# Moving VectorE's picks behind the wide maxima and ScalarE's widening behind the scores in a graph attention kernel

## The chip, the cores and the metric

The kernel runs on one core of one Trainium2 chip. The metric is the device time of one execution in microseconds, and the median over several runs is what counts. PE is TensorE, DVE is VectorE, ACT is ScalarE, POOL is GpSimd and SP is SyncE; a line such as L2286 is that line of the kernel before.

## The reference

A graph of 12,500 nodes and 212,500 edges (self loops included, edges sorted by destination) passes through one attention layer with two heads and edge features, and then through three plain attention layers. The change is in the plain layers and in a judgement made once before them. A plain layer computes:

```python
h = x @ W
alpha_s = h @ a_src
alpha_d = h @ a_dst
e = alpha_s[src] + alpha_d[dst]
e = jnp.where(e > 0, e, NEG_SLOPE * e)
m = jax.ops.segment_max(e, dst, num_segments=n_nodes)
...
ex = jnp.exp(e - m[dst])
s = jax.ops.segment_sum(ex, dst, num_segments=n_nodes)
alpha = ex / (s[dst] + 1e-16)
out = jax.ops.segment_sum(alpha[:, None] * h[src], dst, num_segments=n_nodes)
return out + b
```

It adds a self loop per node, and a ReLU stands between the layers. The last layer's result is added to a residual.

## The kernel before, in words

**The units.** Each plain layer is the function `plain_layer`, called three times with tables of 67 columns (one that holds 1, 64 features, and the source and destination scores). The edges are cut into units. A unit covers up to 128 consecutive destination nodes and 16 tiles of 128 edges. Its 16 tiles of source rows come in two ways. Four tiles are "kept": one is the unit's own rows (self loops), three hold edges whose source lies among the first 1920 nodes, which rest in SBUF as bfloat16 pieces. The other twelve tiles are fetched by POOL, one indirect DMA of 128 rows each (L2150).

**The picks.** For the kept tiles VectorE builds matrices of zeros and ones from a list of places: `make_picks` compares the list with the node numbers (L2221) and with five block numbers (L2223). TensorE multiplies them with the own rows (L2430) and the pieces (L2434), and ScalarE copies the product into the row buffer (`copy_classes`, L2342). The picks have two buffers, used in turn; the semaphore `picks_used` says that TensorE has read one.

**The round.** Units run in a loop of rounds of four, with a ring of four row buffers. In the round of unit n VectorE goes through these steps, in this written order:

1. `localize` for unit n+2 (L2197) and `build_mask` for unit n+1 (L2203, L2205);
2. the picks for unit n+1 (L2221, L2223);
3. `finish` for the unit two before (L2232 to L2238, in the last layer L2244) and `begin` for unit n (L2261 to L2270);
4. `weigh` for unit n: the maximum over tiles (L2277, L2278, then after the last scores L2280, L2281, L2282), the carried sums (L2251), the leaky step over all 2048 scores (L2286), the unit's maxima made wide (L2290 to L2293), the rescale difference (L2296), and, once TensorE has turned the wide maxima (`max_turned`, L2496), the subtraction of the maximum in three parts (L2300).

ScalarE in the same round widens the destination scores of unit n+2 (`widen_er`, L2336), copies the kept rows (L2342), makes twelve tiles of scores after the first eight gathers and four after the last four (L2363), copies the turned result (L2349), and takes the exponentials behind each part of the subtraction (L2393, L2395). TensorE turns the widened scores (`turn_er`, L2411), spreads edges over destinations (L2419), sums the weighted rows (L2464), and multiplies the picks of unit n+1 after the first eight tiles of its sums.

POOL only gathers: before each unit it waits until the sums of the unit four before are made and the indices are there. SP loads each unit's lists four units ahead, one after the other in one queue.

**The judgement.** While the two-headed layer runs, VectorE lists the edges in 116 fitting units (`Arrangement`). `write_classes` marks per partition whether one of four counts is too large (L1224), TensorE sums the marks over the partitions, and `judge` (L1249 to L1256) sets which list of units the plain layers run: `plain_base`, the first unit, and `plain_last`, the last. The long list that fits any graph has 128 times 139 units.

Of the kernel before, what the change touches and what calls it, by code (L numbers as in the profile page):

```python
# [24 lines left out]
P = 128  # L25
# [4 lines left out]
NB = P  # L30
# [902 lines left out]
class Arrangement:  # L933
# [22 lines left out]
    def place(self, ctx):  # L956
        def sb(tag, shape, dt=F32):
            return ctx.enter_context(self.nc.sbuf_tensor(f"arr_{tag}", shape, dt))
        sem = self.con.sem
        self.tiles = [sb(f"tile{k}", [P, CAP], I32)[:, :] for k in range(4)]  # L960
        self.counts = [sb(f"counts{k}", [P, 3 * BANK * 2], F16)[:, :] for k in range(2)]
        self.loc_out = sb("loc_out", [P, KEPT * P], F16)
        self.first, self.prior, self.span, self.spare = (sb(tag, [P, 1]) for tag in ("first", "prior", "span", "spare"))
        self.first_raw, self.after_raw, self.prior_raw = (sb(tag, [P, 1], I32) for tag in ("fr", "ar", "pr"))
        self.kept, self.left = (sb(tag, [P, 1]) for tag in ("kept", "left"))
        self.bad, self.met = sb("bad", [P, 4]), sb("met", [1, 4])
        self.to_far = sb("to_far", [P, 1])
        self.class_counts = sb("class_counts", [P, KEPT])
        self.class_most = sb("class_most", [P, 1])
        self.near_ints, self.near_floats = sb("near_ints", [P, INTS], I32), sb("near_floats", [P, FLOATS])  # L970
        self.late_ints = sb("late_ints", [P, self.later, INTS], I32)
        self.late_floats = sb("late_floats", [P, self.later, FLOATS])
        self.nice = sb("nice", [1, 1])
        self.rows_loaded, self.late_loaded = sem("arr_rows_loaded"), sem("arr_late_loaded")
        self.late_made, self.late_stored, self.chain = sem("arr_late_made"), sem("arr_late_stored"), sem("arr_chain")
        self.bad_made, self.bad_summed = sem("arr_bad_made"), sem("arr_bad_summed")
# [229 lines left out]
    def write_classes(self, ve):  # L1206
# [5 lines left out]
        for k in range(KEPT):  # L1212
# [6 lines left out]
        step(ve.scalar_tensor_tensor(temp, temp, self.to_far[:, 0:1], valid, ALU.add, ALU.mult))  # L1219
        step(ve.tensor_scalar(self.tiles[3][:, 0:KEPT * P].rearrange("r (k p) -> r k p", k=KEPT), temp,  # L1220
                              float(self.far), None, ALU.add))
        for k, (count, most) in enumerate(((self.kept, LISTED - 1), (self.left, SLOTS), (self.class_most, P),
                                           (self.span, NB - 1))):
            step(ve.tensor_scalar(self.bad[:, k:k + 1], count[:, :], float(most), None, ALU.is_gt))  # L1224
        ve.sem_inc(self.bad_made, 1)

    def beside(self, ve, n):
# [20 lines left out]
    def judge(self, ve, ps_bad):  # L1248

        step, nice = self.step, self.nice[:, :]  # L1250
        ve.wait_ge(self.bad_summed, 1)
        for k in range(4):
            step(ve.tensor_scalar(self.met[:, k:k + 1], ps_bad[:, k:k + 1], 0.0, float(4 << k), ALU.is_gt, ALU.mult))
        step(ve.tensor_reduce(nice, self.met[:, :], AX.X, ALU.add))
        step(ve.memset(self.con.plain_base[:, :], 0))
        step(ve.tensor_scalar(self.con.plain_last[:, :], nice, float(SETS - 1), None, ALU.add))  # L1256

    def store(self, gp, stored):

# [29 lines left out]
def heads_layer(nc, con, name, units, src, dst, table, out, middle, edge_attr, attn_l, w_out, arrange):  # L1289
# [17 lines left out]
    with ExitStack() as ctx:  # L1307
# [107 lines left out]
        with nc.Block() as block:  # L1415
# [114 lines left out]
            def _(ve):  # L1530
# [158 lines left out]
                weigh_rows(n, RING - 1, weighted_last)  # L1689
                finish(n, step)  # L1690
                finish(ve.snap(n + 1), step, last_ps)
                arrange.judge(ve, ps_scores[0:1, 0:4])

            @block.scalar
            def _(ac):
# [105 lines left out]
            def _(te):  # L1801
# [99 lines left out]
                project(te.snap(n + 1))  # L1901
                te.wait_ge(scores_copied, n + 1)
                te.wait_ge(arrange.bad_made, 1)
                te.matmul(ps_scores[:, 0:4], con.ones[:, :], arrange.bad[:, :]).then_inc(arrange.bad_summed, 1)


def plain_layer(nc, con, name, arrange, selector, table, out, bias, residual=None, last_rows=None, next_weights=None):
# [16 lines left out]
    with ExitStack() as ctx:  # L1924
# [15 lines left out]
        def after(h):  # L1940
            return (h + 1) % RING

        def before(h, by=1):
            return (h - by) % RING
# [84 lines left out]
        with nc.Block() as block:  # L2029
# [135 lines left out]
            def _(ve):  # L2165
# [107 lines left out]
                def weigh(i, n, h, step):  # L2273
# [20 lines left out]
                                     max_unit[:, :].to_broadcast([NB, P]), ALU.max).then_inc(max_made, 1)  # L2294
                    ve.wait_ge(max_made, n + 1)
                    step(ve.tensor_tensor(rescale[h][:, :], max_before[:, :], max_wide[:, 0:1], ALU.subtract))  # L2296
                    ve.wait_ge(max_turned, n + 1)
                    for cols in PARTS:
                        count = cols.stop - cols.start
# [5 lines left out]
                make_shift(0, 0)  # L2305
                build_mask(0, 0, step)
                make_picks(0, 0)
                cut_spans()
                with ve.Fori(0, rounds) as i:
                    for h in range(RING):  # L2310
# [1 line left out]
                        step = own_steps(ve, chain, ve.snap(n * STEPS))  # L2312
                        localize(i + (h >= RING - 2), before(h, 2))
                        build_mask(n + 1, after(h), step)
                        ve.wait_ge(picks_used, n + 1)
                        make_picks(i + (h == RING - 1), after(h))
                        finish(i, h, n, step)
                        begin(i, h, step)
                        weigh(i, n, h, step)
# [8 lines left out]
            def _(ac):  # L2328
# [16 lines left out]
                def copy_result(n):  # L2345

                    if residual is None:
                        ac.wait_ge(result_turned, n + 2)
                        ac.activation(result_t[:, :], ps_result, ACT.Relu).then_inc(result_copied, 1)  # L2349
# [26 lines left out]
                with ac.Fori(0, rounds) as i:  # L2376
                    for h in range(RING):
                        n = ac.snap(RING * i + h)
                        widen_er(n + 2, i + (h >= RING - 2), before(h, 2))
                        copy_classes(n, h)  # L2380

                        ac.wait_ge(mask_made, n + 1)
# [3 lines left out]
                        score(h, range(KEPT, EARLY)).then_inc(scored_early, 1)  # L2386
                        ac.wait_ge(gathered_last[h], 16 * (Q - EARLY) * i + 16 * (Q - EARLY))
                        score(h, range(EARLY, Q)).then_inc(scored, 1)
                        copy_result(n)

                        for k, cols in enumerate(PARTS):
# [177 lines left out]
```

## Time and profile before

| what | value |
|---|---|
| median of 3 runs | 8422.7 us (8417.76 to 8425.44) |
| the profiled execution | 8420.64 us |
| its span, first to last instruction | 8418.9 us |
| granted TensorE clock, mean | 0.613 |
| first gather of the three plain layers | 2536.0, 4494.0 and 6454.0 us |
| DMA over the span | 45 GB/s |

The plain layers take the time from about 2536 us to the end. Busy times are sums over a whole span or window. The idle time of an engine is put down to what released it; "issue" means that the profile shows nothing that the engine waited for. In a timeline the columns are the start in us, the time in us, the engine, the line, the operation, the tiles written and read, the number of instructions merged, and in brackets the idle time before it with its releaser.

### The profile page before, as it was taken

The numbers are of one execution on the slowest core, as the hardware profiler recorded it, in microseconds if no ns is written. First come the engines' busy times: TensorE is split into PE (matmuls) and PEld (weight loads), VectorE is DVE, ScalarE is ACT, GpSimd is POOL, SyncE is SP. The second block draws the span as 40 slices with busy tenths as digits, with TensorE's granted clock in tenths as the row PEclk, the third lists the DMA queues.
The fourth block names the chain that finished last, engine by engine and source line by source line (L and its number), as shares of the span: only waits on it lengthen the run. The fifth ranks groups of instructions, "written<-read, shape, count | busy, mean of one in ns | idle before, by whom it ended". The sixth has DMA issues, their size and how long they took to land. (4 is left out here: it accounts for less than half of the span.)

```text
span 8418.9 us, 166045 instructions
## 1 busy us (share of the span) xinstructions
PE 6126.8 (73%) x42561; PEld 5518.3 (66%) x42912; DVE 7297.4 (87%) x15869; ACT 4525.5 (54%) x13224; POOL 6245.7 (74%) x5871
## 2 busy tenths in 40 slices
PE   3666767677766777777776777777776777777777
PEld 3666656666655666776666666676666666766666
DVE  7888888888888888888887988888887888888888
ACT  3777767777754555455453444444443444444444
POOL 5777767777727777777776777777776777777776
PEclk9666666666666566555555555555555555555555
DMA  3222222222222222222222222222222222222222
GB/s 92 51 54 52 52 48 55 51 55 59 57 77 48 38 38 37 38 37 38 38 37 40 38 37 38 38 37 38 38 37 40 42 41 42 41 42 42 41 42 37
DMA packets 599847, 379.87 MB, mean 45 GB/s; under 512 B 435013, under 2 KB 488016, under 8 KB 599479
## 3 DMA queue, kind: packets, MB, share of 16 engines
q0 software_dynamic: 187248, 203.53, 14.8%
q1 hardware_dynamic: 404561, 169.88, 8.8%
q10 hardware_dynamic: 7952, 5.60, 0.2%
q14 instruction: 67, 0.54, 0.0%
q8 instruction: 19, 0.31, 0.0%
HBM read 345.43 MB, written 33.90 MB: 45 GB/s over the span
## 5 line engine op out<-in xcount | busy, mean ns | idle before, releaser
L2150 POOL DMA_INDIRECT plain_rows_in<-table,plain_idx x4176 | 4520.7, 1083 | 1401.6 <-issue 1385.7
L2464 PEld LDWEIGHTS plain_ps_sums<-plain_rows_in,plain_prob 128*128 128x128 f32 x11232 | 2245.9, 298 | 184.6 <-issue 65.4
L2464 PE MATMUL plain_ps_sums<-plain_rows_in,plain_prob 128*128 128x65 f32 x11232 | 2272.2, 382 | 31.1 <-ACT plain_prob L2393 20.8
L2393 ACT ACTIVATE plain_prob<-plain_prob 128x512 f32<-128x512 f32 (+1 forms) x1044 | 795.0, 772 | 2641.5 <-DVE plain_prob L2300 2603.9
L1518 POOL DMA_INDIRECT heads_rows_in<-h_in,heads_idx x1664 | 1700.2, 1022 | 657.1 <-issue 589.2
L2363 ACT ACTIVATE plain_prob<-plain_mask,plain_rows_in 128x128 f32<-128x128 f32 x5568 | 1680.9, 387 | 211.3 <-DMA plain_rows_in<-table,plain_idx 172.4
L2300 DVE TENSOR_TENSOR plain_prob<-plain_prob,plain_ps_max 128x512 f32<-128x512 f32 (+1 forms) x1044 | 841.2, 861 | 325.3 <-PE plain_ps_max L2496 325.3
L2434 PEld LDWEIGHTS plain_ps_out<-plain_pieces,plain_picks 128*128 128x128 bf16 x15795 | 953.8, 136 | 0.0
L2434 PE MATMUL plain_ps_out<-plain_pieces,plain_picks 128*128 128x66 bf16 x15795 | 937.4, 245 | 0.0
L2205 DVE SCALAR_TENSOR_TENSOR plain_mask<-plain_ps_apart,plain_er_rows 128x2048 f32<-128x2048 f32 x351 | 804.5, 2292 | 16.8 <-PE plain_ps_apart L2419 4.5
L2286 DVE SCALAR_TENSOR_TENSOR plain_prob<-plain_prob 128x2048 f32<-128x2048 f32 x348 | 795.7, 2286 | 0.0
L1833 PE MATMUL heads_ps_turn<-ident,heads_onehot 128*128 128x128 f32 x1680 | 349.6, 377 | 568.2 <-ACT heads_pairs_t L1711 449.3
L1759 ACT ACTIVATE heads_masked<-heads_mask,heads_scores_sum 128x128 f32<-128x128 bf16 x2496 | 748.9, 389 | 0.0
L1833 PEld LDWEIGHTS heads_ps_turn<-ident,heads_onehot 128*128 128x128 f32 x1680 | 278.7, 196 | 592.5 <-issue 466.8
L2430 PE MATMUL plain_ps_out<-plain_own,plain_self_pick 128*128 128x66 f32 x702 | 238.2, 443 | 571.7 <-DVE plain_picks L2223 560.9
L2411 PE MATMUL plain_ps_max<-ident,plain_er_wide 128*128 128x128 f32 x354 | 139.2, 393 | 679.6 <-DVE plain_column_max L2282 616.8
L2430 PEld LDWEIGHTS plain_ps_out<-plain_own,plain_self_pick 128*128 128x128 f32 x702 | 175.3, 310 | 635.4 <-issue 322.1
L2411 PEld LDWEIGHTS plain_ps_max<-ident,plain_er_wide 128*128 128x128 f32 x354 | 58.9, 166 | 767.3 <-issue 767.3
L1854 PEld LDWEIGHTS heads_ps_acc<-heads_weighted,heads_onehot 128*128 128x128 f32 x3328 | 520.5, 248 | 11.4 <-issue 11.4
L1854 PE MATMUL heads_ps_acc<-heads_weighted,heads_onehot 128*128 128x130 f32 x3328 | 520.8, 330 | 8.7 <-DVE heads_weighted L1635 8.7
L2419 PE MATMUL plain_ps_apart<-selector,plain_dst_local 128*128 128x512 bf16 x1065 | 451.7, 553 | 55.8 <-issue 48.6
L2223 DVE TENSOR_SCALAR plain_picks<-plain_locs,block_ids 128x384 bf16<-128x384 f16 x1755 | 451.2, 322 | 0.0
(386 smaller groups left out, 9846.3 us busy)
## 6 DMA issues: line engine op xcount, KB each, us to landing
plain_rows_in<-table,plain_idx POOLq DMA_INDIRECT x4176
heads_edges<-in_edge_attr SPq DMA_DIRECT2D x108, 512.0 KB
plain_locs<-arranged_loc SPq DMA_DIRECT2D x360, 128.0 KB
heads_rows_in<-h_in,heads_idx POOLq DMA_INDIRECT x1664
plain_own<-table SPq DMA_DIRECT2D x360, 33.5 KB
table<-plain_out_sb SPq DMA_DIRECT2D x232, 33.5 KB
plain_dst_ids<-arranged_dst SPq DMA_DIRECT2D x360, 8.0 KB
plain_unit_par<-plain_floats SPq DMA_DIRECT2D x360, 1.0 KB
```

The source lines that it names most:

```text
L1518: gp.indirect_dma_start(rows_in[h][:, t, :], None, table[:, :], bass.IndirectOffsetOnAxis(ap=idx[h][:, t:t + 1], axis=0)).then_inc(gathere ...
L1759: ins = ac.activation(tile, mask[:, t, :], ACT.Identity, bias=scores_sum[:, t, hd:hd + 1])
L1833: ins = te.transpose(ps_turn[g % TURN_BANKS][0:NB, t % GROUP * P:(t % GROUP + 1) * P], onehot[h][:, t, :], con.ident[:, :])
L1854: ins = te.matmul(acc_ps, onehot[h][:, t, :], weighted[:, t, :], start=t == 0, stop=t == Q - 1)
L2150: gp.indirect_dma_start(rows_in[h][:, t, :], None, table[:, :], bass.IndirectOffsetOnAxis(ap=idx[h][:, t - KEPT:t - KEPT + 1], axis=0)).th ...
L2205: ve.scalar_tensor_tensor(mask[h % 2][:, :, :], apart, 0.0, bcast(er_rows[:, :], 1, Q), ALU.not_equal, ALU.subtract).then_inc(mask_made, 1)
L2286: step(ve.scalar_tensor_tensor(tile[:, :, :], tile[:, :, :], SLOPE, tile[:, :, :], ALU.mult, ALU.max))
L2300: ve.tensor_tensor(tile[:, cols, :], tile[:, cols, :], bcast(max_row, 1, count), ALU.subtract).then_inc(logits_made, 1)
L2363: ins = ac.activation(prob[h % 2][:, t, :], mask[h % 2][:, t, :], ACT.Identity, bias=rows_in[h][:, t, src_at:src_at + 1], scale=-BIG)
L2393: ac.activation(prob[h % 2][:, cols, :], prob[h % 2][:, cols, :], ACT.Exp).then_inc(weights_made, 1)
L2434: ins = te.matmul(ps_class[:, c + 1, :], picks[h % 2][:, b, c * P:(c + 1) * P], pieces[:, k, c * BLOCKS + b, :], start=b + k == 0, stop=b ...
L2464: ins = te.matmul(sums[h % 2], prob[h % 2][:, t, :], rows_in[slot][:, t, 0:part], start=t == 0, stop=t == Q - 1)
```

## The change

`make_picks` leaves its place between `build_mask` and `finish`. It now runs inside `weigh`, between the rescale difference and the wait for the turned maxima, and makes the picks of unit n+2 instead of n+1. So one more set is made before the loop. `widen_er` moves from the head of ScalarE's round to behind the last scores. The four marks of a bad fit are added up in one column; `judge` sees one sum, multiplies by whether the edges are sorted, and sets the first and the last unit from that factor: a good fit gives 0 and 115, a bad one the long list.

```diff
-        self.kept, self.left = (sb(tag, [P, 1]) for tag in ("kept", "left"))
-        self.bad, self.met = sb("bad", [P, 4]), sb("met", [1, 4])
+        self.kept, self.left, self.bad = (sb(tag, [P, 1]) for tag in ("kept", "left", "bad"))
...
-        for k, (count, most) in enumerate(((self.kept, LISTED - 1), (self.left, SLOTS), (self.class_most, P),
-                                           (self.span, NB - 1))):
-            step(ve.tensor_scalar(self.bad[:, k:k + 1], count[:, :], float(most), None, ALU.is_gt))
+        bad = self.bad[:, :]
+        step(ve.tensor_scalar(bad, self.kept[:, :], float(LISTED - 1), None, ALU.is_gt))
+        for count, most in ((self.left, SLOTS), (self.class_most, P), (self.span, NB - 1)):
+            step(ve.scalar_tensor_tensor(bad, count[:, :], float(most), bad, ALU.is_gt, ALU.add))
...
-        for k in range(4):
-            step(ve.tensor_scalar(self.met[:, k:k + 1], ps_bad[:, k:k + 1], 0.0, float(4 << k), ALU.is_gt, ALU.mult))
-        step(ve.tensor_reduce(nice, self.met[:, :], AX.X, ALU.add))
-        step(ve.memset(self.con.plain_base[:, :], 0))
-        step(ve.tensor_scalar(self.con.plain_last[:, :], nice, float(SETS - 1), None, ALU.add))
+        step(ve.tensor_scalar(nice, ps_bad, 0.0, self.con.is_sorted[0:1, 0:1], ALU.is_equal, ALU.mult))
+        step(ve.tensor_scalar(self.con.plain_base[:, :], nice, -float(P), float(P), ALU.mult, ALU.add))
+        step(ve.tensor_scalar(self.con.plain_last[:, :], nice, float(SETS - P * self.later),
+                              float(P * self.later - 1), ALU.mult, ALU.add))
...
                     step(ve.tensor_tensor(rescale[h][:, :], max_before[:, :], max_wide[:, 0:1], ALU.subtract))
+                    ve.wait_ge(picks_used, n + 1)
+                    make_picks(i + (h >= RING - 2), before(h, 2))
                     ve.wait_ge(max_turned, n + 1)
...
                 make_picks(0, 0)
+                make_picks(0, 1)
                 cut_spans()
...
                         build_mask(n + 1, after(h), step)
-                        ve.wait_ge(picks_used, n + 1)
-                        make_picks(i + (h == RING - 1), after(h))
                         finish(i, h, n, step)
...
                         n = ac.snap(RING * i + h)
-                        widen_er(n + 2, i + (h >= RING - 2), before(h, 2))
                         copy_classes(n, h)
...
                         score(h, range(EARLY, Q)).then_inc(scored, 1)
+                        widen_er(n + 2, i + (h >= RING - 2), before(h, 2))
                         copy_result(n)
```

The matmul that sums the marks over the partitions (L1904) has one column instead of four.

## Rows read from the trace of the kernel before

**Rows 1.** The page's first part: busy us, share of the span, instructions.

```profile
PE 6126.8 (73%) x42561; PEld 5518.3 (66%) x42912; DVE 7297.4 (87%) x15869; ACT 4525.5 (54%) x13224; POOL 6245.7 (74%) x5871
```

**Rows 2.** Gathers by line, one plain layer each: duration min/median/max ns, first and last start.

```profile
L2150 POOL DMA_INDIRECT plain_rows_in<-table,plain_idx x1392: 940/944/2677, 2536.0 to 4466.6; - x199
...
L2150 POOL DMA_INDIRECT plain_rows_in<-table,plain_idx x1392: 939/944/2671, 4494.0 to 6426.5; - x199
...
L2150 POOL DMA_INDIRECT plain_rows_in<-table,plain_idx x1392: 940/944/2627, 6454.0 to 8380.3; - x199
```

**Rows 3.** Waits in the second plain layer: total us, times, longest us.

```profile
POOL plain_rows_in L2150 <- issue: 447.9, 1384, 26.4
...
DVE plain_prob L2300 <- PE plain_ps_max L2496: 105.0, 116, 1.3
...
DVE plain_top L2280 <- ACT plain_prob L2363: 41.2, 64, 0.9
```

**Rows 4.** Timeline of the second layer, POOL's gathers around one unit.

```profile
5011.97 0.94 POOL L2150 DMA_INDIRECT plain_rows_in<-table,plain_idx  x1 [0.30 <-issue]
...
5014.47 1.41 POOL L2150 DMA_INDIRECT plain_rows_in<-table,plain_idx  x1 [0.30 <-issue]
...
5016.18 1.15 POOL L2150 DMA_INDIRECT plain_rows_in<-table,plain_idx  x1 [0.30 <-issue]
...
5017.63 0.94 POOL L2150 DMA_INDIRECT plain_rows_in<-table,plain_idx  x1 [0.30 <-issue]
...
5018.88 1.89 POOL L2150 DMA_INDIRECT plain_rows_in<-table,plain_idx  x1 [0.30 <-issue]
...
5028.57 0.94 POOL L2150 DMA_INDIRECT plain_rows_in<-table,plain_idx  x1 [0.30 <-issue]
```

**Rows 5.** The same timeline, VectorE.

```profile
5005.65 2.42 DVE L2300 TENSOR_TENSOR plain_prob<-plain_prob,plain_ps_max 128x512 f32<-128x512 f32 x3 [1.25 <-PE plain_ps_max L2496]
...
5014.37 0.69 DVE L2277 TENSOR_TENSOR plain_top<-plain_prob 128x512 f32<-128x512 f32 x1 [0.16 <-DVE plain_self_row L2270]
...
5015.82 0.69 DVE L2280 TENSOR_TENSOR plain_top<-plain_top,plain_prob 128x512 f32<-128x512 f32 x1
...
5017.67 2.29 DVE L2286 SCALAR_TENSOR_TENSOR plain_prob<-plain_prob 128x2048 f32<-128x2048 f32 x1
...
5020.84 0.16 DVE L2296 TENSOR_TENSOR plain_rescale<-plain_max_before,plain_max_wide 128x1 f32<-128x1 f32 x1
...
5027.29 0.28 DVE L2221 TENSOR_SCALAR plain_self_pick<-plain_locs,node_id 128x128 f32<-128x128 f16 x1
...
5028.78 0.27 DVE L2232 SCALAR_TENSOR_TENSOR plain_acc<-plain_acc_in,plain_rescale,plain_ps_sums 128x65 f32<-128x65 f32 x1
```

**Rows 6.** The same timeline, ScalarE.

```profile
5009.27 0.30 ACT L2336 ACTIVATE plain_er_wide<-plain_own 128x128 f32<-128x128 f32 x1
5009.47 0.38 ACT L2342 ACTIVATE plain_rows_in<-plain_ps_out 128x264 f32<-128x264 f32 x1
...
5009.95 3.61 ACT L2363 ACTIVATE plain_prob<-plain_mask,plain_rows_in 128x128 f32<-128x128 f32 x12
...
5014.43 1.28 ACT L2363 ACTIVATE plain_prob<-plain_mask,plain_rows_in 128x128 f32<-128x128 f32 x4 [0.87 <-DMA plain_rows_in<-table,plain_idx]
```

**Rows 7.** Timeline of the third layer, VectorE and POOL.

```profile
7512.31 1.30 DVE L2223 TENSOR_SCALAR plain_picks<-plain_locs,block_ids 128x384 bf16<-128x384 f16 x5
7513.38 1.05 POOL L2150 DMA_INDIRECT plain_rows_in<-table,plain_idx  x1 [0.30 <-issue]
...
7519.38 2.28 DVE L2286 SCALAR_TENSOR_TENSOR plain_prob<-plain_prob 128x2048 f32<-128x2048 f32 x1
...
7519.86 2.61 POOL L2150 DMA_INDIRECT plain_rows_in<-table,plain_idx  x1 [0.30 <-issue]
```

**Rows 8.** The late maximum by line, third layer.

```profile
L2280 DVE TENSOR_TENSOR plain_top<-plain_top,plain_prob x116: 691/692/693, 6483.3 to 8396.7; 128x512 f32<-128x512 f32 x116
```

**Rows 9.** The judgement's first steps, by tile.

```profile
L1253 DVE TENSOR_SCALAR arr_met<-heads_ps_scores x4: 146/147/147, 2436.5 to 2437.1; 1x1 f32<-1x1 f32 x4
```

More of the change, by code:

```diff
@@ L1691, in _ @@
                 finish(ve.snap(n + 1), step, last_ps)
-                arrange.judge(ve, ps_scores[0:1, 0:4])
+                arrange.judge(ve, ps_scores[0:1, 0:1])
             @block.scalar
@@ L1903, in _ @@
                 te.wait_ge(arrange.bad_made, 1)
-                te.matmul(ps_scores[:, 0:4], con.ones[:, :], arrange.bad[:, :]).then_inc(arrange.bad_summed, 1)
+                te.matmul(ps_scores[:, 0:1], con.ones[:, :], arrange.bad[:, :]).then_inc(arrange.bad_summed, 1)
 def plain_layer(nc, con, name, arrange, selector, table, out, bias, residual=None, last_rows=None, next_weights=None):
```

## The prediction

> **What bounds the kernel now.** On the page the engines' row comes first: VectorE (DVE) is busy for 87% of the span, GpSimd (POOL) for 74% [rows 1]. That points at VectorE, from whose round the change takes a piece. The idle column of the gathers corrects it. In the second of the three attention layers POOL issues 1392 gathers [rows 2], and the time it sits idle before them is put down to "issue" (447.9 us in 1384 cases, one of 26.4 us at the layer's start, the rest 0.30 us each): it hardly ever waits for data [rows 3]. A gather takes 0.94 us (median), so an undisturbed one costs 0.94 + 0.30 = 1.25 us and twelve cost 14.97 us. Yet first and last start over 1391 intervals, times twelve, give 16.66, 16.67 and 16.62 us a unit in the three layers [rows 2]. The rest is stretch, and the timeline shows whose: the gather of 5014.47 ends at 5015.88, that of 5016.18 at 5017.33, that of 5018.88 at 5020.77 [rows 4]; on VectorE the early maximum L2277 ends at 5015.06, the late one L2280 at 5016.51, the leaky step L2286 at 5019.96 [rows 5]. Each time the gather ends 0.81 or 0.82 us after the VectorE instruction. A gather that starts inside one of these instructions is held until it ends, and one that starts just before (5017.63, against L2286 at 5017.67) passes.
>
> This closes a loop in the second layer. The last gather of a unit ends at 5012.91 (5011.97 + 0.94) [rows 4]. ScalarE starts the last four scores at 5014.43 after waiting 0.87 us for that DMA [rows 6]. L2280 follows at 5015.82, 2.91 us after the gather's end, and L2286 ends 4.14 us later [rows 5]. The fifth gather of the next unit, held by L2286, ends 0.81 us after it, and seven undisturbed gathers bring the next last one to 5028.57 + 0.94, 8.74 us later [rows 4]. 2.91 + 4.14 + 0.81 + 8.74 = 16.60 us, the measured round. VectorE waits in it twice: for the scores (41.2 us in 64 units) and for the transposed maxima before L2300 (105.0 us in 116 units, 0.91 on average) [rows 3]. The third layer differs: a gather is held by L2286 there too (it starts at 7519.86 and ends at 7522.47, 0.81 after L2286) [rows 7], but L2280 has its scores long before: its last start, 8396.7, is 15.5 us after the last gather's end [rows 2, 8]. There the gathers follow VectorE's round.
>
> **The change, part by part.** (1) Picks: L2221 and five L2223 take 1.49 us from the first start to the next work (5027.29 to 5028.78) [rows 5]. They leave the place between mask and finish and enter the gap between L2296 and L2300, which is 0.16 + 0.91 = 1.07 us on average from start to start [rows 3, 5]. The new gap is 0.16 for L2296, some 0.04 for the hand-over (steps of 0.15 us that wait for each other start 0.2 apart [rows 9]) and 1.49: 1.69 us. So VectorE's own round shrinks by 1.49 - (1.69 - 1.07) = 0.87 us and its exponentials start up to 0.6 us later. In the first two layers the loop above contains neither place, so the 0.87 us become a longer wait for the scores: 0. The added waits are met: the picks of the unit two on go into the buffer whose matmuls ran a round earlier, and its list of places was fetched four units ahead. Behind the waiting picks stand only VectorE's subtraction and ScalarE's exponentials.
>
> (2) The third layer: with a shorter round VectorE uses up its delay behind the gathers until the same loop closes. The rounds are then the loop's (16.60 to 16.67 instead of 16.62, +3 us over 115), but at the end it stands 2.9 instead of 15.5 us behind the last gather: -12.6. Together -9 us.
>
> (3) Picks beside gathers: the picks now run right behind L2286, where the sixth and seventh gathers start. A gather beside picks took 1.05 us at 7513.38 (0.11 over) [rows 7]; that of 5028.57, begun before the last pick's end, 0.94 [rows 4]. Bounds: nothing, and 0.11 a unit or 38 us; a gain is excluded except in the third layer, which pays now. I take 0.03 a unit, nearer to the undisturbed row, since a gather begun ahead of a short pick passes it: +10 us. The Trainium skill, "SBUF — State Buffer", section "Who interferes with whom", says that an instruction of the picks' kind in a two-port mode locks GpSimd out for its whole length. By that rule the sum would be the third rival's upper price; the rows show a tenth of a microsecond, because each of the six is short.
>
> (4) ScalarE: widening the destination scores costs 0.20 us of the queue (5009.27 to 5009.47) [rows 6]. Moved behind the last score it lies in ScalarE's wait for the next subtraction; the transpose that reads it waits for the column maximum, which comes after L2280. If the exponentials start 0.6 us later and this 0.20 is saved, the first twelve scores end 0.4 us later at most, within ScalarE's 0.87 us wait for the gather [rows 6]: 0. If that cover were gone, the second rival follows.
>
> (5) Judging: seven small steps become three, at 0.2 us a step [rows 9]: -0.8, taken as -1. One more set of picks per layer before the loop (1.5 us) delays VectorE's start, while the first gathers set the pace: 0. No DMA is added, and none changes its place in SP's or POOL's queue.
>
> Sum: 0 - 9 + 10 + 0 - 1 = 0. The profiled execution took 8420.6 us, its span is 8418.9, and the median of the runs is 2.1 above it at 8422.7. I predict 8422.
>
> **The rivals.** *VectorE is the bound after all.* For it: it is the busiest engine [rows 1]. Then 0.87 x 348 = 303 us go: 8120. Against it: POOL has no gap to give, and VectorE waits for ScalarE. It needs gathers that shorten with VectorE's round.
>
> *The loop opens.* If VectorE runs behind by more than 0.54 us, an otherwise unheld fifth gather (due at 5012.91 + 0.30 + 4 x 1.25 = 5018.21) passes before L2286, and the sixth is the one held: 1.25 us less in the loop. The round is then that of VectorE and ScalarE: 7.91 us from L2300 to the twelfth score (5005.65 to 5013.56) less 0.20, then 0.03 hand-over, 1.45 to L2280, 1.85 to L2286, 3.17 to L2296, 0.20 to 0.30 and 1.49 for the picks: 15.9 to 16.0 us [rows 5, 6]. Gathers keep up with a round of 0.81 + 0.30 + 10 x 1.25 + 2.29 = 15.90 us or more, plus whatever else holds one. That is nearly a tie. Price: 0.7 x 115 = 80 us a layer; in the first two less some 13, because VectorE would still stand some 15.5 instead of 2.9 us behind at the layer's end: 67 each, so 8288, and in all three about 8210. I hold the tie to fall short, since a pick or an early maximum needs to hold only one gather for 0.1 us.
>
> *Picks hold the gathers (slower).* Place: the sixth and seventh gather, behind L2286. Decides: a gather that starts inside a pick instead of ahead of it. At 0.11 to 0.2 us a unit 38 to 70 us: up to 8490. By the full length of the picks, 1.49 x 348 = 520 us: 8940; no row shows a gather held over several picks, so this end has 0.01 of the chance.
>
> *The fourth gather is caught (slower).* It passes L2286 by 0.04 us [rows 4, 5]. If the moved maxima put it behind, it waits 2.2 us: one gather, 1.25 us, more in the loop, over some 300 units 375 us: 8800. But its start is tied to L2280's end when that holds the third, and 1.25 us earlier when nothing does.
>
> *The fit is judged no.* Then each layer runs the long list of 17,792 units instead of 116, over a hundred times as long. The before run shows 116 units a layer, as the test for a good fit gives; only the sortedness factor is new.
>
> **How the numbers follow.** Forecast 0.57, loop open 0.22, VectorE-bound 0.05, picks 0.10, fourth gather 0.05, judged no 0.01. About 0.2%, 17 us, is what a measurement can tell from no change; within the forecast the bounds of its terms (-24, with the loop at 16.60 throughout and no pick in the way, to +28, with 0.11 a unit) leave 0.08 faster and 0.07 slower. Faster: 0.08 + 0.22 + 0.05 = 0.35; same 0.42; slower: 0.07 + 0.10 + 0.05 + 0.01 = 0.23. The range runs from the open loop in two layers (8285) to the picks at a moderate hold (8465); left out are 0.05 VectorE-bound, 0.05 of the open loop, 0.06 of the two rare losses, 0.03 of the picks. The forecast's own range is 8398 to 8450.
>
> **What would show it.** Right: POOL idle only for issue, about 16.6 us a unit; VectorE's wait before L2300's subtraction near zero and its wait for the scores over 0.6 us a unit, now in the third layer too; L2280 2.9 us behind the last gather at the end of every layer. Wrong: a round near 16.0 with no wait for scores (loop open), gathers beside picks over 1.05 us, or a round near 17.9.

## The result and the profile after

The kernel after took 8451.0 us (8 runs, 8445.3 to 8458.5) beside 8422.4 for the kernel before on the same chip: a ratio of 1.0034, 95% interval 1.0023 to 1.0045. It is slower by 28.6 us. The profiled execution took 8450.4 us, its span is 8448.8. Most lines moved up by one: L2149 are the gathers, L2276, L2277 and L2279 the maxima, L2285 the leaky step, L2222 the block picks, L2301 the subtraction.

Waits of the second layer of after (total us, times, longest us), to be held against [rows 3]:

```profile
POOL plain_rows_in L2149 <- issue: 450.4, 1388, 27.7
...
ACT plain_prob L2363 <- DMA plain_rows_in<-table,plain_idx: 98.9, 103, 1.2
DVE plain_top L2279 <- ACT plain_prob L2363: 91.5, 103, 1.1
DVE plain_top L2276 <- ACT plain_prob L2363: 68.4, 116, 2.3
```

POOL's waits are still put down to issue (1388 of 1392 gathers). VectorE's wait for the turned maxima (105.0 us) is gone, its wait for the late scores (L2279) has grown from 41.2 to 91.5 us, and a wait for the early scores (L2276, 68.4 us) is new: the round became shorter on VectorE and turned into waiting. The gathers and the late maximum by line, layer by layer (duration min/median/max ns, first and last start; under the late maximum its idle time in us, times):

```profile
L2149 POOL DMA_INDIRECT plain_rows_in<-table,plain_idx x1392: 940/945/2678, 2538.0 to 4485.9; - x199
...
L2279 DVE TENSOR_TENSOR plain_top<-plain_top,plain_prob x116: 691/692/694, 2571.5 to 4489.7; 128x512 f32<-128x512 f32 x116
...
L2149 POOL DMA_INDIRECT plain_rows_in<-table,plain_idx x1392: 940/945/2617, 4514.6 to 6456.6; - x199
...
L2279 DVE TENSOR_TENSOR plain_top<-plain_top,plain_prob x116: 691/692/758, 4548.4 to 6460.5; 128x512 f32<-128x512 f32 x116
...
L2149 POOL DMA_INDIRECT plain_rows_in<-table,plain_idx x1392: 940/945/2677, 6485.7 to 8423.7; - x199
...
L2279 DVE TENSOR_TENSOR plain_top<-plain_top,plain_prob x116: 691/693/765, 6516.4 to 8427.5; 128x512 f32<-128x512 f32 x116
its engine sat idle before it (us, times) until:
  ACT plain_prob L2363: 100.8, 105
```

The third layer is read so: VectorE's round is (8427.5 - 6516.4) / 115 = 16.62 us, and without the 100.8 / 115 = 0.88 us of waiting its **own round** is 15.74 us; before it was 16.64, with no such wait in that layer [rows 8]. The own round leaves out this one wait alone; waits for ScalarE's early scores and for TensorE are in it. The last gather ends at 8424.6, and the last late maximum starts 2.9 us later: VectorE's distance behind the gathers, here called the lead, is used up, as forecast. Before, it was 15.2 us and not the 15.5 of the prediction, since the last gather of that layer took 1.15 us and ended at 8381.5. But the gathers' round is 1938.0 / 1391 x 12 = 16.72 us where it was 16.62 [rows 2].

The late maxima of the first two layers before:

```profile
L2280 DVE TENSOR_TENSOR plain_top<-plain_top,plain_prob x116: 691/692/715, 2568.1 to 4470.6; 128x512 f32<-128x512 f32 x116
...
L2280 DVE TENSOR_TENSOR plain_top<-plain_top,plain_prob x116: 691/692/694, 4526.3 to 6430.3; 128x512 f32<-128x512 f32 x116
```

From first gather to last late maximum the layers of after took 1951.7, 1945.9 and 1941.8 us; before, 1934.6, 1936.3 and 1942.7 [rows 2, 8]. So +17.1, +9.7 and -0.9; the remaining 4.0 us of the span's 29.9 lie between and around the layers.

In what follows a unit is **closed** when its late maximum starts less than 3.7 us behind the end of its last gather; mostly the loop of the prediction binds it then. (In the second and third layer of after VectorE waits for the late scores in 208 of 210 closed units, in the first only in 64 of 98.) A layer counts as closed from its first such unit. Before, the three layers are closed from unit 46, unit 22 and never; after, from unit 18, 12 and 10, so 305 of the 345 intervals instead of 162. A unit of the closed kind in the second layer of after, timeline of POOL (start, time, line, idle before):

```profile
5506.39 1.26 POOL L2149 DMA_INDIRECT plain_rows_in<-table,plain_idx  x1 [0.30 <-issue]
5507.95 1.29 POOL L2149 DMA_INDIRECT plain_rows_in<-table,plain_idx  x1 [0.30 <-issue]
...
5510.80 1.89 POOL L2149 DMA_INDIRECT plain_rows_in<-table,plain_idx  x1 [0.30 <-issue]
5512.99 0.94 POOL L2149 DMA_INDIRECT plain_rows_in<-table,plain_idx  x1 [0.30 <-issue]
5514.24 1.06 POOL L2149 DMA_INDIRECT plain_rows_in<-table,plain_idx  x1 [0.30 <-issue]
5515.61 0.94 POOL L2149 DMA_INDIRECT plain_rows_in<-table,plain_idx  x1 [0.30 <-issue]
5516.86 0.96 POOL L2149 DMA_INDIRECT plain_rows_in<-table,plain_idx  x1 [0.30 <-issue]
5518.12 0.94 POOL L2149 DMA_INDIRECT plain_rows_in<-table,plain_idx  x1 [0.30 <-issue]
```

The timeline of VectorE in the same stretch:

```profile
5506.14 0.69 DVE L2277 TENSOR_TENSOR plain_top<-plain_top,plain_prob 128x512 f32<-128x512 f32 x1
5507.74 0.69 DVE L2279 TENSOR_TENSOR plain_top<-plain_top,plain_prob 128x512 f32<-128x512 f32 x1 [0.91 <-ACT plain_prob L2363]
...
5509.59 2.29 DVE L2285 SCALAR_TENSOR_TENSOR plain_prob<-plain_prob 128x2048 f32<-128x2048 f32 x1
...
5513.26 1.23 DVE L2222 TENSOR_SCALAR plain_picks<-plain_locs,block_ids 128x384 bf16<-128x384 f16 x5
5514.40 2.41 DVE L2301 TENSOR_TENSOR plain_prob<-plain_prob,plain_ps_max 128x512 f32<-128x512 f32 x3
5516.73 0.27 DVE L2196 TENSOR_SCALAR plain_dst_local<-plain_dst_ids,plain_unit_par 16x128 bf16<-16x128 int32 x1
```

Two maxima, the leaky step, the last pick and the localizing each hold one gather, which ends 0.81 or 0.82 us after they do (5506.83 + 0.81 = 5507.64; 5514.49 + 0.81 = 5515.30). The holds of the second, third and fifth gather were there before; those of the seventh (1.06) and ninth (0.96) are new in the closed loop.

### The profile page after: what moved, and what is told of

Same layout as the page of the kernel before. It is cut to its first block and busy times, and to the rows that moved or that the text cites. A ratio compares the mean times of both kernels' runs of the same rounds, so it can differ in the third digit from the quotient of the medians.

```text
span 8448.8 us, 166149 instructions
## 1 busy us (share of the span) xinstructions
PE 6297.3 (75%) x42912; PEld 5647.4 (67%) x42912; DVE 7312.5 (87%) x15883; ACT 4520.8 (54%) x13224; POOL 6281.6 (74%) x5871
## 5 line engine op out<-in xcount | busy, mean ns | idle before, releaser
L2149 POOL DMA_INDIRECT plain_rows_in<-table,plain_idx x4176 | 4558.9, 1092 | 1403.7 <-issue 1399.5
L2464 PEld LDWEIGHTS plain_ps_sums<-plain_rows_in,plain_prob 128*128 128x128 f32 x11232 | 2389.3, 315 | 290.6 <-ACT plain_prob L2393 143.5
L2464 PE MATMUL plain_ps_sums<-plain_rows_in,plain_prob 128*128 128x65 f32 x11232 | 2409.0, 398 | 113.6 <-ACT plain_prob L2393 106.2
L2434 PE MATMUL plain_ps_out<-plain_pieces,plain_picks 128*128 128x66 bf16 x15795 | 920.2, 243 | 0.0
L2301 DVE TENSOR_TENSOR plain_prob<-plain_prob,plain_ps_max 128x512 f32<-128x512 f32 (+1 forms) x1044 | 837.0, 854 | 0.0
L2285 DVE SCALAR_TENSOR_TENSOR plain_prob<-plain_prob 128x2048 f32<-128x2048 f32 x348 | 796.2, 2288 | 0.0
L2419 PE MATMUL plain_ps_apart<-selector,plain_dst_local 128*128 128x512 bf16 x1416 | 652.9, 614 | 0.0
L1853 PEld LDWEIGHTS heads_ps_acc<-heads_weighted,heads_onehot 128*128 128x128 f32 x3328 | 524.9, 250 | 12.3 <-issue 12.3
L2222 DVE TENSOR_SCALAR plain_picks<-plain_locs,block_ids 128x384 bf16<-128x384 f16 x1770 | 459.0, 323 | 0.0
L2279 DVE TENSOR_TENSOR plain_top<-plain_top,plain_prob 128x512 f32<-128x512 f32 x348 | 241.3, 693 | 250.9 <-ACT plain_prob L2363 248.3
L2276 DVE TENSOR_TENSOR plain_top<-plain_prob 128x512 f32<-128x512 f32 x348 | 241.0, 693 | 205.6 <-ACT plain_prob L2363 201.7
```

The source lines that it names most:

```text
L1853: ins = te.matmul(acc_ps, onehot[h][:, t, :], weighted[:, t, :], start=t == 0, stop=t == Q - 1)
L2149: gp.indirect_dma_start(rows_in[h][:, t, :], None, table[:, :], bass.IndirectOffsetOnAxis(ap=idx[h][:, t - KEPT:t - KEPT + 1], axis=0)).th ...
L2285: step(ve.scalar_tensor_tensor(tile[:, :, :], tile[:, :, :], SLOPE, tile[:, :, :], ALU.mult, ALU.max))
L2301: ve.tensor_tensor(tile[:, cols, :], tile[:, cols, :], bcast(max_row, 1, count), ALU.subtract).then_inc(logits_made, 1)
L2419: ins = te.matmul(ps_apart[:, at:at + BANK], dst_local[h % 2][:, :], selector[:, at:at + BANK])
L2434: ins = te.matmul(ps_class[:, c + 1, :], picks[h % 2][:, b, c * P:(c + 1) * P], pieces[:, k, c * BLOCKS + b, :], start=b + k == 0, stop=b ...
```

## The experiments

Theory at first: the picks, in their new place, hold the seventh gather, and that is the loss. Rivals: the widening or the judgement makes it; or the later exponentials do. When the first run fell out against the theory, a second was formed: what counts is in how many units the loop is closed, and how long its round then is. All ratios are to the kernel before, run in turn on the same chip.

| run | ratio, 95% interval | own round, third layer, us | closed from unit, by layer |
|---|---|---|---|
| before | 1 | 16.64 | 46, 22, never |
| after | 1.0034 (1.0023 to 1.0045) | 15.74 | 18, 12, 10 |
| picks only | 0.9999 (0.9990 to 1.0008) | 15.94 | 47, 17, 16 |
| rest only | 1.0004 (0.9995 to 1.0013) | 16.66 | 21, 23, never |
| picks early | 0.9998 (0.9989 to 1.0007) | 15.53 | 15, 11, 10 |
| split, after | 0.9855 (0.9840 to 0.9870) | 16.10 | never |
| after again | 1.0028 (1.0017 to 1.0039) | 15.74 | 17, 12, 9 |
| picks only again | 1.0004 (0.9995 to 1.0013) | 15.94 | 67, 19, 23 |
| split, before | 0.9965 (0.9951 to 0.9978) | 16.76 | never |
| after, VectorE delayed | 0.9884 (0.9869 to 0.9900) | 16.12 | never |
| after, ScalarE delayed | 0.9993 (0.9984 to 1.0002) | 15.92 | never, 30, 16 |
| split and early | 0.9765 (0.9752 to 0.9779) | 15.82 | never |
| split and shared | 0.9729 (0.9715 to 0.9742) | 16.09 | never |
| after, delayed twice | 1.0080 (1.0067 to 1.0094) | 16.49 | never |

**Picks only.** The kernel before with the diff's hunks that touch `make_picks`, nothing else.

> Only the picks move (with the extra set ahead of the loop); the widening and the judgement stay as before. Theory (picks in their new place hold the seventh gather of a unit by 0.1 us in three units of four): the whole loss is here, 8447 to 8453 us, seventh gather 0.07 to 0.08 us over its 0.944 on average in the units whose late maximum stands 2.9 us behind the last gather. Rival (the widening behind the scores or the judgement makes the loss): 8420 to 8426.

Measured: 8412.7 us beside 8412.6. The seventh gather is over its 0.944 by 0.065 to 0.08 us in the closed units, as expected, yet the time is that of before. The theory that the hold alone makes the loss fell.

**Rest only.** The kernel after with the picks in their old place.

> The widening moves and the judgement changes; the picks stay where they were. Theory: 8417 to 8425, the gathers' excess by place as before. Rival: 8445 to 8452.

Measured: 8419.2 us, not told apart from before (8412.6; 1.0004, 0.9995 to 1.0013). So neither part loses alone, and the rival fell too.

**Picks early.**

```diff
+                    ve.wait_ge(picks_used, n + 1)
+                    make_picks(i + (h >= RING - 2), before(h, 2))
                     ve.wait_ge(max_made, n + 1)
                     step(ve.tensor_tensor(rescale[h][:, :], max_before[:, :], max_wide[:, 0:1], ALU.subtract))
-                    ve.wait_ge(picks_used, n + 1)
-                    make_picks(i + (h >= RING - 2), before(h, 2))
```

> The kernel after, with the picks directly behind the wide maxima and ahead of the rescale difference, so some 0.33 us earlier against the gathers. In the kernel after the sixth gather starts 1.12 and the seventh 2.37 us behind the leaky step's end, the last pick ends at 2.60. Theory (a pick holds a gather that starts in it): the last pick ends near 2.3, so the seventh gather is free (0 over 0.944); the sixth, at 1.12, now meets the first block's pick (some 1.0 to 1.3) and is held by 0 to 0.06 us. Time: 8425 with 0, 8443 with 0.06. Rival (the loss comes from exponentials that start later, wherever the picks stand against the gathers): seventh gather unchanged at 0.07 to 0.08, 8450.

Measured: 8412.0 us. The sixth gather is 0.04 us over on average, the seventh exactly free. A closed unit in its second layer, timeline of POOL, the fifth to seventh gather:

```profile
5508.21 1.89 POOL L2149 DMA_INDIRECT plain_rows_in<-table,plain_idx  x1 [0.30 <-issue]
5510.41 0.96 POOL L2149 DMA_INDIRECT plain_rows_in<-table,plain_idx  x1 [0.30 <-issue]
5511.68 0.95 POOL L2149 DMA_INDIRECT plain_rows_in<-table,plain_idx  x1 [0.30 <-issue]
```

And of VectorE, the block picks:

```profile
5510.24 1.23 DVE L2222 TENSOR_SCALAR plain_picks<-plain_locs,block_ids 128x384 bf16<-128x384 f16 x5
```

The first pick ends near 5510.5 and holds the gather of 5510.41 for a moment; the last ends at 5511.47, ahead of the gather of 5511.68. The closed round is 16.57 and 16.60 us in the second and third layer (16.72 and 16.70 in after). Of that, some 0.08 us are the free seventh gather; 0.06 us are not the edit's: in the runs of this first group ScalarE starts the late scores 1.47 us behind the last gather's end, in the profiles of before and after and in the next group 1.53. The landing favours this kernel over the kernel before, which is closed in fewer units: 0.06 x (309 - 162) is some 9 us, an estimate from the closed intervals of this trace and of the trace of before. So at the landing of the other groups the ratio would be near 1.001. Though the loop is closed in as many units as in after, most of the loss is gone, so the holds behind the leaky step are a part of it. The rival of the later exponentials fell: the picks still stand ahead of the subtraction.

**The leaky step split, in after.**

```diff
-                    step(ve.scalar_tensor_tensor(tile[:, :, :], tile[:, :, :], SLOPE, tile[:, :, :],
-                                                 ALU.mult, ALU.max))
+                    for t in range(0, Q, 4):
+                        part_t = tile[:, t:t + 4, :]
+                        ins = ve.scalar_tensor_tensor(part_t, part_t, SLOPE, part_t, ALU.mult, ALU.max)
+                    step(ins)
```

> The kernel after, with the leaky step as four instructions of 512 columns in place of one of 2048 (some 0.06 us more for each of three, estimated from the 0.69 us of a 512-column maximum and the 2.29 us of the leaky step). Theory (a gather is held to the end of the one instruction that it starts in, and that hold closes the loop of gathers, scores and leaky step): the fifth gather's excess falls from 1.0 to 0 to 0.5 us, the loop opens, and the round becomes VectorE's and ScalarE's own, 15.8 + 0.2 = 16.0 us; less some 12 us a layer in which the last units drain: 8200 to 8270. Rival (the hold lasts until VectorE stops using the port, over all four pieces): fifth gather held 1.2 us, 8470 to 8510. Rival (the bound is elsewhere): 8450 plus nothing.

Measured: 8294.0 us. Timeline of VectorE, second layer, one leaky step:

```profile
5501.85 2.54 DVE L2287 SCALAR_TENSOR_TENSOR plain_prob<-plain_prob 128x512 f32<-128x512 f32 x4
```

The timeline of POOL beside it:

```profile
5501.81 0.94 POOL L2149 DMA_INDIRECT plain_rows_in<-table,plain_idx  x1 [0.30 <-issue]
5503.06 0.94 POOL L2149 DMA_INDIRECT plain_rows_in<-table,plain_idx  x1 [0.30 <-issue]
5504.31 0.94 POOL L2149 DMA_INDIRECT plain_rows_in<-table,plain_idx  x1 [0.30 <-issue]
```

Three gathers pass beside 2.54 us of the same work, now in four instructions. The loop never closes, the round is VectorE's own (16.43, 16.09 and 16.10 us in the three layers), and 119 us go against before. It is 24 us above the expected range: the first layer's round is longer than the 16.0 us expected, and VectorE stands 24 us behind the last gather at the end of each layer, 21 more than in the closed loop, where 12 were reckoned.

**After again, and picks only again.** Both side by side, to see whether after's loss is real beside picks only.

> The kernel after, unchanged, beside the two kernels below. On the chip of the first four runs the last gather's rows reach ScalarE's scores 1.47 us behind the gather's end in the closed loop; in the runs of before and after it was 1.53 to 1.54. Theory A (the cost of the change depends on this landing time, because after spends 305 units in the closed loop and before 162; with 1.47 the change costs nothing): within 0.1% of before here, about as the kernel with the picks alone. Theory B (the loss is real on every chip and needs both moves together): 25 to 32 us above before, 0.3 to 0.4%, and as far above the kernel with the picks alone. Either way the seventh gather 0.07 to 0.08 us over 0.944 in the closed loop.

> Only the picks move, once more, beside the kernel after on the same chip. Theory A: equal to after within 8 us. Theory B: 25 us below after.

Measured: 8449.3 and 8426.9 us, before 8425.8. Beside each other, after loses and picks only does not: the loss needs both moves, as theory B has it. Theory A was not met as it was meant: the scores start 1.53 us behind the last gather's end in both traces, so whether after would lose at 1.47 is open. The trace of picks only is of an execution of 8414.0 us, 12.9 below the median. Its third layer, the late maximum:

```profile
L2280 DVE TENSOR_TENSOR plain_top<-plain_top,plain_prob x116: 691/691/720, 6487.4 to 8389.6; 128x512 f32<-128x512 f32 x116
its engine sat idle before it (us, times) until:
  ACT plain_prob L2364: 69.3, 92
```

Own round 16.54 - 0.60 = 15.94 us, 0.2 us longer than after's; the widening at the head of ScalarE's queue is what differs. With that the first layer is closed from unit 67 instead of 17, and before that the gathers' round is 16.60 us (over the same 67 units it is 16.85 in after again).

**The leaky step split, in before.** The same edit.

> The kernel before with the leaky step as four instructions of 512 columns. With the split the kernel after took 8294 us, and its round became VectorE's and ScalarE's own. Theory (once no gather is held for long, the round is VectorE's own, and only there do the picks' 0.87 us pay): in before VectorE's own round is 16.2 us in the first two layers and 16.65 in the third; the split adds 0.25 to it, so 16.45, 16.45 and 16.9 us instead of 16.65, 16.65 and 16.62: -23, -23 and +32 us, with some 12 us more at the end of each of the first two layers: 8405 to 8450, 110 to 155 us above the split kernel after. Rival (the gathers' hold is all that matters, with or without the moved picks): 8290 to 8310.

Measured: 8394.1 us, 32 below before and, by the ratios, 93 above split after. With the gathers nearly free, the moves of the change pay: the own round in the second layer is 16.31 us here and 16.09 there. The forecast of 110 to 155 was too high, as the split cost the own round 0.1 and not 0.25 us there.

**VectorE delayed, in after.** Behind the picks, with one step more per unit:

```diff
+                    step(ve.tensor_reduce(pad[0][:, :], con.lag[:, :], AX.X, ALU.max))
```

> The kernel after with one instruction more on VectorE, behind the picks: a maximum over 128 columns of a constant that nobody reads (0.29 us, some 0.25 us of its round). Theory (the loop opens: where VectorE's own round is so long that its leaky step falls behind the fifth gather, the gathers are held less and the round is VectorE's own): own round 15.8 + 0.25 = 16.05 instead of 16.7, with the gathers keeping up: 8300 to 8350, more work and less time. Rival (the added instruction falls into VectorE's wait for the scores): unchanged against after. Rival (it lies on the path): 0.25 x 305 = 76 us slower than after.

Measured: 8325.9 us, 100 below before and 123 below after, by an instruction whose result nobody reads. The second layer's late maximum by line:

```profile
L2280 DVE TENSOR_TENSOR plain_top<-plain_top,plain_prob x116: 691/692/693, 4529.8 to 6392.0; 128x512 f32<-128x512 f32 x116
its engine sat idle before it (us, times) until:
who waited for it (us, times):
```

And POOL's timeline in that layer:

```profile
5503.09 0.95 POOL L2150 DMA_INDIRECT plain_rows_in<-table,plain_idx  x1 [0.30 <-issue]
5504.34 1.89 POOL L2150 DMA_INDIRECT plain_rows_in<-table,plain_idx  x1 [0.30 <-issue]
5506.53 0.94 POOL L2150 DMA_INDIRECT plain_rows_in<-table,plain_idx  x1 [0.30 <-issue]
5507.78 1.05 POOL L2150 DMA_INDIRECT plain_rows_in<-table,plain_idx  x1 [0.30 <-issue]
```

No wait before the late maximum, a round of 1862.2 / 115 = 16.19 us, and per unit a stretch of 1.20 us of the gathers where the closed loop of after has 1.74: the leaky step still holds one, but the maxima hold little. The prediction's rival of the open loop is a real state; after's own round is 0.36 to 0.38 us short of this kernel's in the second and third layer. In the third layer it would not last: the gathers' round of 16.20 us is longer than VectorE's 16.12, and the lead falls from 16.0 to 6.0 us over the layer.

**ScalarE delayed, in after.** A copy of 128 columns that nobody reads, at the head of its round:

```diff
+                        ac.activation(pad[:, :], con.lag[:, :], ACT.Copy)
                         copy_classes(n, h)
```

> The kernel after with a copy of 128 columns that nobody reads at the head of ScalarE's round, where the widening stood (0.20 us of its queue); the real widening stays behind the scores. Theory (the widening matters only through the 0.2 us: without it the own round of ScalarE and VectorE is 15.82 us, VectorE uses up its lead over the gathers by unit 17, 12 and 9 of the layers instead of 67, 19 and 23, and from then on the closed loop with a held seventh gather sets the round): own round 16.0 again, the time of the kernel with the picks alone, 0 to 0.1% above before. Rival (the place of the widening itself delays something, such as TensorE's turn of the widened scores): 0.25 to 0.35% above before, like after.

Measured: 8415.9 us beside 8422.0. The whole loss is gone, with the widening still behind the scores. So it is the 0.2 us at the head of ScalarE's round that matter, not the widening's new place. The scores start 1.53 us behind the last gather's end here too, as in after. The trace, and so the table's row, is of an execution of 8405.7 us, 10 below the median.

**Split and early, split and shared.** Both edits together; then three of the six picks back between mask and finish.

> The kernel after with the leaky step in four instructions and the picks ahead of the rescale difference. Theory (with the gathers free the round is VectorE's and ScalarE's, and the picks' new place shortens it by the 0.22 us that it took off the own round without the split, 15.82 to 15.60): round 15.83 instead of 16.05, ratio to before 0.974 to 0.979. Rival (at 15.8 the gathers, still held by short pieces, become the bound again): ratio 0.984 to 0.988, as with the split alone.

> As the run before, and three of the six picks (the own rows' and two blocks') return to their place between mask and finish, for the unit whose other three were made a round earlier. There VectorE waits 0.4 to 0.5 us for ScalarE's early scores in the split kernel. Theory (these 0.68 us leave the path from the maxima to the subtraction and fall mostly into that wait): round 15.83 - 0.45 = 15.4 us, ratio 0.955 to 0.965. Rival (the gathers' own round, 14.97 and some 0.5 to 1.0 us of holds, ends it earlier): ratio 0.970 to 0.978, POOL never waiting for TensorE's sums.

Measured: 8225.2 and 8192.8 us beside 8422.0. The first has the ratio that was forecast; of its rounds (16.25, 15.91 and 15.82 us) only the third layer's is the 15.83 expected. The second gained 0.004 instead of the 0.012 to 0.022 that its theory gives over the first. Its rounds are 0.27 and 0.23 us shorter in the first two layers and 0.26 us longer in the third. The rival's ratio came out and its reason did not; the waits over the whole span name another one:

```profile
PE plain_ps_out L2440 <- DVE plain_picks L2228: 366.1, 290, 2.6
...
POOL plain_rows_in L2149 <- PE plain_ps_sums L2474: 143.5, 158, 2.6
```

TensorE waits for the picks that are completed late, and POOL still has time to wait for TensorE's sums. That this wait costs the missing gain was not tried. This is the fastest kernel of the study, 229 us below before.

**Delayed twice.** Two such instructions instead of one.

> The kernel after with two instructions more on VectorE behind the picks, each a maximum over 128 columns of a constant, the second waiting for the first (some 0.33 us more than with one). Theory (with one, the loop is open and the round is VectorE's own, 16.1 to 16.2 us; every further delay is then paid in full): 8326 + 0.33 x 348 = 8440 us, ratio to before 0.999 to 1.005, no wait for the scores, lead of VectorE over 3 us throughout. Rival (the first delay helped by moving something against the gathers by chance, and the second moves it back): closed loop again, 8440 to 8460 with VectorE waiting for the scores 0.3 us or more a unit.

Measured: 8486.9 us beside 8417.9. The loop stays open and the own round of the third layer rises by 0.37 us, as the theory says; the 47 us more than forecast go with a wait that no theory had, shown by VectorE's waits from 4600 to 6300 us, in the second layer, whose round rises by 0.70 us (16.19 to 16.89):

```profile
DVE plain_top L2277 <- ACT plain_prob L2366: 48.2, 75, 0.7
DVE plain_dst_local L2197 <- issue: 46.6, 25, 2.2
```

Once in four units VectorE idles 1.9 us at the head of its loop in this layer, and nothing visible releases it. Its cause stays open.

## Why the prediction was wrong

The bound was named rightly: in after, too, POOL's waits are put down to issue, VectorE waits for the scores, and the closed loop sets the round. The forecast of no change failed at two steps: step (1) put the picks' move at nothing in the first two layers, as if the loop were closed in all their units, and step (3) put the picks' hold too low.

The traces give the sizes. Each stretch of a gather beyond 0.944 us is put down to the VectorE instruction that ended 0.82 us before the gather did. Summed over the three layers, in us:

| held by | before | after | after again | picks only again | after, ScalarE delayed |
|---|---|---|---|---|---|
| the maxima | 127.6 | 203.5 | 202.2 | 122.6 | 118.1 |
| the leaky step | 437.4 | 378.1 | 377.2 | 430.1 | 421.8 |
| picks | 11.1 | 26.1 | 24.5 | 20.8 | 23.4 |
| `localize` | 0.0 | 5.2 | 5.3 | 4.9 | 5.0 |
| all, with the rest | 578.5 | 616.8 | 618.4 | 583.3 | 571.3 |

- **Step (1), picks moved, 0.** The picks alone shrank the own round in the third layer by 0.70 us (16.64 to 15.94) where 0.87 was forecast; the widening took off another 0.20. All went into the wait, as said. But "the loop above contains neither place" took the first two layers as closed throughout. They were open for 46 and 22 units, and the change moved that point to 18 and 12. No term of the sum had this. In the first layer the first 46 units take 16.54 us each before and 16.84 after, 14 of the layer's 17 us. Maxima and leaky step together hold 11 us more there, and 1 us more in the second layer.
- **Step (2), third layer, -9.** The lead went from 15.2 to 2.9 us, worth 12.3; the closed round there is 16.70 and not 16.60 to 16.67, over 105 units 3 to 11 us. Measured -0.9.
- **Step (3), picks beside gathers, +10.** This term was mis-sized: 0.03 us a unit was taken, because "a gather begun ahead of a short pick passes it". In the 296 closed units whose fifth gather is held, the seventh starts 2.37 us behind the leaky step's end, beside the last pick, and is held by 0.10 us in 220 of them. The mean over a layer's closed units is 0.07 to 0.08, together 22 us. Over all units the picks hold 26 us in after where they held 11 before, 15 more; `localize`, which the sum did not have, adds 5. The upper bound of 38 us stood.
- **Step (4), widening, 0.** It failed together with (1). Alone it cost nothing that could be told; on top of the moved picks its 0.2 us brought the own round from 15.94 to 15.74, the loop closed earlier, and the time rose by 22 us (8449.3 against 8426.9). Giving 0.2 us back on ScalarE took the loss away. The argument that the saving "lies in ScalarE's wait" was not enough: the own round did shorten, and a longer wait is what a closed loop looks like.
- **Step (5), judgement and extra picks, -1.** Not measured apart from the widening; together 1.0004 (0.9995 to 1.0013). Outside the layers the span grew by 4.0 us.

So the forecast missed by some 12 us in (1), 5 in (3), 5 for `localize` and 5 outside the layers; the rest is within 2 us.

Of the rivals, "picks hold the gathers" had the right place, and its time (8460 to 8490) was somewhat high. "The loop opens" did not happen: its own round was put at 15.9 to 16.0 us and came out 0.1 to 0.2 shorter in the last two layers. The delayed kernel shows what it gives, 8326 where 8288 and 8210 were worked out. The full lock over all picks did not come: no hold by the picks in the five traces of the table is over 0.13 us, so a gather was held by one pick, never by several.

What is shown: lengthening the own round by 0.2 us on ScalarE removes the loss, and freeing the seventh gather removes most of it. The table tells how the two divide between after again and picks only again: 27 of the 35 us by which their gathers differ lie with the maxima and the leaky step, where an earlier closing shows, and only 4 with picks and `localize`. (The executions that were traced differ by 35 us, the medians by 22.) With ScalarE delayed the new holds are still there, 28 us, and the loss is not: the third layer's shorter lead and the open first layer pay for them. Why the irregular own round of before (16.2 us on average in its second layer) closes while the steady 16.19 of the delayed kernel stays open was not tried.

## What to carry to other kernels

Where one engine's transfers are held by another engine's long instructions, saving time on the waiting side may only lock the two together sooner: look how many units already run in the locked state, and what the locked round is. Break the instruction that closes the loop first; here the leaky step in four pieces took the kernel after from 1.003 to 0.986 of before, and then the moves of the change paid (93 us against the kernel before with the same split). When a step is moved on a busy engine, work out against the other engine's phase where each of its instructions lands.

## What was not expected of the hardware

The seventh gather and the last pick meet within some hundredths of a microsecond: over the closed units the gather starts 2.37 us behind the leaky step's end with a standard deviation of 0.004 us, and yet it is held by 0.10 us in 220 units and free in 76. In the free ones the last pick takes 0.37 us (median of 76), in the others 0.31 (median of 220). So one of the two yields, now this one and now that one. The Trainium skill, "SBUF — State Buffer", section "Who interferes with whom", has it that issue order decides who blocks. The trace shows that either can be the one that waits, by 0.10 or 0.06 us; the order it does not show, since the pick's record starts 0.08 us ahead of the gather's in both cases.

Not every long instruction holds. The mask, which has an operand in PSUM, in the closed unit shown above:

```profile
5517.23 2.29 DVE L2204 SCALAR_TENSOR_TENSOR plain_mask<-plain_ps_apart,plain_er_rows 128x2048 f32<-128x2048 f32 x1
```

It runs to 5519.52, and the gather of 5518.12 in its midst takes 0.94 us. In the three layers of after 561 gathers start in a mask at least 0.15 us ahead of its end, and none takes over 0.96 us. Whether the operand in PSUM is the reason was not tried.
